# A two-layer decoder on one core: square's result, the decay sums' refill and the recurrence's store in the first layer

## The reference

```python
x = x + _L0_attn_ref(_layernorm(x), ...)            # m: state space
x = x + _L0_xattn_ref(_layernorm(x), ctx, ctx, ...)  # c: attention on the context
x = x + _L0_ffn_ref(_layernorm(x), ...)              # r: recurrence

# m, for each head h (in the kernel a 128 x 128 matrix of decays stands for the scan)
decay = jnp.exp(A * dt_t)
state = state * decay + (x_t * dt_t) * B_t
y_t = einsum(state, C_t)
y = (y + x_part * D) * silu(z)
y = y * rsqrt(mean(y * y) + EPS) * norm_w            # the mean needs the sum of squares
out = einsum(y, out_proj_w)

# r
ft = sigmoid(xt @ wf.T + c @ uf.T + bf); it = sigmoid(...); gt = tanh(...)
c = ft * c + it * gt
h = tanh(xt @ wo.T + c_final @ uo.T + bo)
```

## Time and profile before

| | |
|---|---|
| median of 3 runs | 3414.84 us (3406.63 to 3415.68) |
| the profiled execution, its own time | 3411.43 us |
| its span, first to last instruction | 3409.5 us |
| PE busy / DVE / ACT / POOL, share of the span | 90% / 81% / 66% / 44% |
| the stretch of the loop of "layer0" | about 230 to 1835 us |
| one step of it | 26.98 us (1003.31 to 1030.29 us) |
| granted TensorE clock, mean over the span | 0.967 |

### The profile page before, as it was taken

One profiled execution on the slowest core, in us unless ns is written; L12 is line 12 of the kernel. 1 busy time (PEld: TensorE's weight loads), 2 busy tenths in 40 slices (PEclk: granted clock), 3 DMA queues, 4 the chain that ended last, 5 costly groups with the idle time before them and its releaser, 6 DMA issues. The chain is left out here.

```text
span 3409.5 us, 95859 instructions
## 1 busy us (share of the span) xinstructions
PE 3084.8 (90%) x27055; PEld 2664.0 (78%) x27056; DVE 2775.2 (81%) x8725; ACT 2260.3 (66%) x8248; POOL 1514.0 (44%) x5113
## 2 busy tenths in 40 slices
PE   6699999999999999999998699989898999499998
PEld 4578888888888888888886577777777777387998
DVE  5588888888888888888885588888888887687776
ACT  4467777777777777777775477777777777143333
POOL 1244444545444544445452155555555554133333
PEclk8789999999999999999999799999999999699999
DMA  6111111111111111111110200000000000023443
GB/s 190 37 36 50 44 41 41 41 48 47 41 41 41 42 47 46 41 41 41 48 48 14 61 20 15 18 15 18 17 17 18 15 19 13 4 103 121 131 136 90
DMA packets 123391, 161.87 MB, mean 47 GB/s; under 512 B 27331, under 2 KB 94832, under 8 KB 123312
## 3 DMA queue, kind: packets, MB, share of 16 engines
q1 hardware_dynamic: 111056, 126.37, 12.7%
q0 software_dynamic: 12256, 34.53, 2.8%
HBM read 102.85 MB, written 61.53 MB: 48 GB/s over the span
## 5 line engine op out<-in xcount | busy, mean ns | idle before, releaser
L380 POOL TENSOR_TENSOR tiny<-tiny 128x1 f32<-128x1 f32 x3456 | 776.0, 225 | 799.1 <-DVE tiny L367 558.3
L806 ACT ACTIVATE work<-bank,att 128x128 f32<-128x128 f32 x2048 | 722.0, 378 | 57.7 <-DVE att L796 51.8
L806 ACT ACTIVATION_READ_ACCUMULATOR work<-bank,att 128x1 f32 x2048 | 445.0, 217 | 0.0
L796 DVE TENSOR_REDUCE att<-bank 128x4 f32<-128x512 f32 x512 | 333.8, 683 | 47.1 <-PE bank L789 47.1
L825 PE MATMUL bank<-const,work 128*128 128x128 f32 x2048 | 318.1, 279 | 31.8 <-ACT work L806 26.1
L789 PEld LDWEIGHTS bank<-work 32*128 32x128 f32 x4096 | 254.0, 189 | 107.0 <-issue 74.7
L1286 DVE SCALAR_TENSOR_TENSOR work<-work,small 128x127 f32<-128x127 f32 (+2 forms) x1152 | 317.5, 345 | 16.0 <-ACT work L1126 10.7
L789 PE MATMUL bank<-work 32*128 32x128 f32 x4096 | 302.7, 286 | 21.1 <-ACT work L1171 2.5
L825 PEld LDWEIGHTS bank<-const,work 128*128 128x128 f32 x2048 | 239.5, 142 | 74.8 <-ACT work L806 58.7
L380 POOL TENSOR_TENSOR tiny<-tiny,const 128x1 f32<-128x1 f32 x1152 | 250.6, 218 | 90.3
L185 PE MATMUL bank<-w1r,workr 128*128 (+2 forms) x802 | 267.5, 333 | 0.5 <-issue 0.2
(11 more groups left out here) (357 smaller groups left out, 8472.8 us busy)
## 6 DMA issues: line engine op xcount, KB each, us to landing
work<-decay_sums SPq DMA_DIRECT2D x64, 512.0 KB, 3.7
work<-pair_rows SPq DMA_DIRECT2D x91, 258.0 KB
pair_rows<-extra SPq DMA_DIRECT2D x128, 182.0 KB
work<-in_ctx SPq DMA_DIRECT2D x128, 128.0 KB, 2.1
x_res<-in_x POOLq DMA_DIRECT2D x8, 1024.0 KB, 17.5
recurrence_out<-r_xo_ SPq DMA_DIRECT2D x64, 128.0 KB, 1.7
work<-recurrence_out SPq DMA_DIRECT2D x64, 128.0 KB
out_dram<-work POOLq DMA_INDIRECT x91, 2.5
```

Of the source, the lines that this page charges most:

```text
L380: e.tensor_tensor(out_, a_, b_, ALU.add if b_ is three_halves else ALU.mult)\
L796: e.tensor_reduce(a_nm[:, 4 * g:4 * g + 4], sc_banks[g % 2][:, :].rearrange("p (h k) -> p h k", k=P), AX.X, ALU.max, negate=True).then_inc ...
L806: last = e.activation(Pb[g % 2][:, c * P:c * P + P], sc_banks[g % 2][:, c * P:c * P + P], ACT.Exp, bias=a_nm[:, 4 * g + c:4 * g + c + 1], ...
```

## The change

Square writes its unread result to `m_zg_`, the gate's buffer, in place of the first half of `m_E`. The refill `load_sums` no longer waits for `m_ss`, only for the products. In SP's step the recurrence's store moves from behind the refill of the sums to the end, behind the context load and the three blank stores, and its lag is 5 in place of 4, so SP's pipeline runs to lag 5.

```diff
                 def load_sums(b):
 
                     if past(b): e.wait_ge(S["m_y"], 2 * b)
-                    if past(b): e.wait_ge(S["m_ss"], b)
...
                     b = i
                     if live(b):
                         load_sums(b)
-                    b = i - 4
-                    if live(b):
-                        store_output(b)
                     b = i
                     if live(b):
                         load_context(b)
                     b = i
                     if live(b):
                         blank_rows(b)
+                    b = i - 5
+                    if live(b):
+                        store_output(b)
 
                 e.wait_ge(S["p_stored"], 16)
                 e.wait_ge(S["blank_ready"], 2)
-                pipeline(e, 4, step)
+                pipeline(e, 5, step)
...
                 def m_square(b):
                     e.wait_ge(S["m_y2"], b + 1)
                     if past(b): e.wait_ge(S["m_rs"], b)
-                    e.activation(m_E[:, 0:4, :].rearrange("p h t -> p (h t)"), m_y_, ACT.Square, accum_out=m_ss_)\
+                    e.activation(m_zg_, m_y_, ACT.Square, accum_out=m_ss_)\
                         .then_inc(S["m_ss"], 1)
```

## The result

The changed kernel took 3500.47 us (median of 4 runs, 3495.54 to 3503.76), the kernel before in the same comparison 3415.26: a ratio of 1.0257, 95% interval 1.0244 to 1.0271. It is slower, as forecast, but by 85 us instead of 41, and outside the range. The profiled execution took 3503.76 us, 92 more than that of before, and 92 is what its steps have to account for.

A forecast was written before the change was run, and what follows sets the result against it. It took a ring of work through PE, with about 1 us of air in a 26.98 us step, as the bound. 68 - 27 = +41 us on 3414.84 gave 3457 us, range 3425 to 3495.

The forecast's parts named there:

- PE's stall ahead of c_project: In the loop, c_project on PE starts 1.15 us late each step: 68 us more over 59 steps.
- the early refill's gain: Refill issued 4.1 us earlier, DVE's wait for the sums gone, 0.45 us a step gained: 27 us less.
- fall of the clock: Ruled out: 1.2 us more air in 28 leaves PE over 92% busy, so no cost was counted.
- Square's target and the removed wait: Square's new output address and the refill's dropped wait for `m_ss`: nothing in the loop from either.
- The new chain: c_transpose, over SP's context load, blank rows and store, to ACT's copy: copy 1.25 us late, then take_inverse and c_project.
- the 0.1 of slack ahead of c_project: Between take_inverse's end and c_project's start, less release: about 0.1 us, cutting the copy's 1.25 us delay to 1.15.
- That is 0.45 us of the 1.19: Of DVE's 1.19 us wait in the step read, only 0.45 is gained, as L1119 waits for PE's projection.
- it gains 0.6 there at most: DVE at residual L1348 is held by POOL's Newton steps, ending at 1013.09, so gains at most 0.6 us.
- The third rival: Store lands late behind the blank rows: +24 us (3481) up to +118 (3575); chance 0.11.
- The first rival: The delay from c_transpose to ACT's copy is hidden and only the gain is left: 3388 us; chance 0.09.

The follow-up runs named there:

- the store second: Changed kernel with the lag-5 store directly behind the refill, ahead of the wait for c_tr: ratio 0.9998 to the kernel before.
- the swap: Against the run with the store second, DVE's second half of the relative sums put ahead of m's residual: 3397.02 us, ratio 0.9968 to the kernel before.

## Why the prediction missed

| term, us over 59 steps | predicted | measured |
|---|---|---|
| PE's stall ahead of c_project | +68 (1.15 a step) | +73 (27.94 - 26.70 = 1.24) |
| the early refill's gain | -27 (0.45) | -5 by the profiles (26.79 - 26.70 = 0.09), none to be seen in the medians |
| fall of the clock | 0 | +26 (28.39 - 27.94 = 0.45) |
| sum | +41 | +94 in the profiles, +85 in the medians |

**Square's target and the removed wait: right.** Nothing for either, shown by the two runs that take them apart from the store.

**The new chain: right in kind and close in size.** Copy, take_inverse, c_project, each with the wait that was named. Counted from the start of c_transpose, the copy began at 6.42 us in place of 5.18, so 1.24 late (1.25 predicted), and c_project 1.24 late (1.15 predicted): the 0.1 of slack ahead of c_project was not there. C_project starts 0.15 us behind the end of take_inverse here (1021.47 to 1021.62) and 0.14 before, so what I took for slack was release time.

**"That is 0.45 us of the 1.19": wrong by a factor of five.** Two readings failed. The step that I read, 1003 to 1030, is 26.98 us long, and the mean is 26.79: its refill landed among the latest. The residual L1348 starts 3.39 us behind c_turn_qk in it (1013.69 less 1010.30), and 3.20 on average over 23 steps between 600 and 1200 us. And "it gains 0.6 there at most" counted POOL's Newton steps to their end only; with the store second, L1347 starts 0.24 us behind that end (1011.99 to 1012.23), 3.16 behind c_turn_qk:

```profile
1011.80 0.19 POOL L380 TENSOR_TENSOR tiny<-tiny 128x1 f32<-128x1 f32 x1
1012.23 0.48 DVE L1347 SCALAR_TENSOR_TENSOR x_res<-bank,tiny,x_res 128x256 f32 x1 [0.76 <-POOL tiny L380]
```

So of DVE's 0.97 us of wait all but a few hundredths was hidden behind POOL already. The start of the convolution, counted in the same way, moved from 6.96 to 6.83. What I had as a cap for DVE alone was the bound of the chain; the taps, which I took for it, bind 0.1 us later, as the swap shows.

**"A fall of the clock is no case of mine": wrong.** I judged by PE's busy share of the step, over 92%. That share held (1302 of 1400 us are 93%), and the clock fell all the same, in 14 of 48 steps, behind a single standstill of 1.05 us. The step that failed is the reason given for putting this term at nothing: a mean over the step says nothing of one gap in it. Filled with transposes, the same gap costs no fall. This and the gain are the two steps that failed, they are of about the same size (26 and 22 us), and they add up. Without the fall the result would have been 3474, with the full gain 3478, both inside the range.

**The third rival** (a late landing behind the blank rows) was rightly kept out of the sum, since the store landed in 1.7 us. What spared the store was the small third store between it and the large ones; without that it took 2.5 us, and two experiments ran into it.

**The first rival** needed a chain shorter by 1.1 us. One that is 3.1 us shorter does take the loss away, and what is left is within 5 us of nothing.

## What to carry to other kernels

A transfer that was off the critical path can enter it when it is moved behind a wait in its queue: ask which wait it now stands behind, when that one is released within the step, what is issued in between, and who waits for the buffer's release. When a wait of an engine is to be removed, look for the second releaser that comes just behind the first one, with its release time, and take the distances from the mean of many steps instead of from one. A stall on a busy TensorE can cost more than itself: here 1.05 us of it brought 0.45 us a step on top by the clock. Work that filled it, or a stall of 0.75 us, gave the clock back.

## What was not expected of the hardware

- The granted clock fell to half behind a short standstill in a stream that is otherwise dense (PE's other wait of each step, 0.7 us ahead of c_out, is there in the kernel before too, without a fall). By PE's wait ahead of c_project: 0.75 us, in 0 of 49 steps; 1.05 us, in 14 of 48; 1.3 us, in 22 of 48; 1.57 us, in 23 of 47; and with the 1.05 us filled with transposes, in 0 of 49. A fall cost 1.5 us in the changed kernel (29.47 less 27.94), 0.86 to 1.55 with the longest stall. The Trainium skill ("TensorE: Matmul & The Clock Gate", section on the clock's oscillation in real kernels) tells of waits for DMAs between groups of matmuls that bring the half clock back in each turn; the trace agrees in kind, for waits much shorter than those of its example, and only in some of the turns. What decides in which step it falls was not tried.
- The same 128 KB store lands in 1.7, 1.9, 2.5 or 3.4 us, by what stands directly ahead of it in the queue: nothing or the small store; the context load; two stores of 182 KB; the refill of 512 KB as written.
- VectorE's residual starts 0.24 us behind the end of GpSimd's last Newton step, while ScalarE's L1118 starts 0.03 us behind what it waits for on TensorE (1012.41 to 1012.44, with the store second). SyncE's context load starts 0.03 us behind c_transpose in the earlier trace rows, and 0.16 in the loop after the change (1015.01 to 1015.17).
